# A state-space scan and a mixture of experts on one core: dt's sum moves to TensorE, an eighth of one product to GpSimd, and the set-up is reordered

## The chip, the core and the metric

One core of a Trainium2 chip runs the whole program in one launch. The metric is device time in microseconds, from the program's start to its end. The engines are TensorE (PE), VectorE (DVE), ScalarE (ACT), GpSimd (POOL) and SyncE (SP, which only issues DMAs). Each runs its own instruction stream in program order; they meet at semaphores.

## What is computed

The input x is 16 sequences of 1024 tokens with 256 features. The output is x plus a selective state-space scan plus a mixture of 8 experts, both on the layer-normalised x.

```python
dt = softplus(einsum('bsd,ed->bse', x, dt_w) + dt_b)
A = -exp(log_A)
b = einsum('bsd,nd->bsn', x, B_w) + B_b      # 32 states
c = einsum('bsd,nd->bsn', x, C_w) + C_b
def step(h, inp):
    x_t, dt_t, b_t, c_t = inp
    A_bar = exp(A[None] * dt_t[..., None])
    h = A_bar * h + (dt_t * x_t)[..., None] * b_t[:, None, :]
    y = einsum('bdn,bn->bd', h, c_t) + D_skip * x_t
    return (h, y)
...
out = relu(einsum('ecd,edh->ech', disp, w1) + b1) ; out = einsum('ech,ehd->ecd', h, w2) + b2
```

Each token goes to its two best experts, up to a capacity of 4096 tokens per expert.

## The kernel before, in words

**Set-up.** The first 125 us normalise all tokens and write them to DRAM (`xn_rows`). Then VectorE finds each token's experts and its place there, and in the stretch from about 168 to 280 us it builds one-hot tiles (`one_hots`, lines L1316 to L1319) that TensorE multiplies into a map of slots to tokens (`map_batch`, L603 and L605). It does so in 32 batches. ScalarE makes the third factor (`low_part`, L848) in the same order, and between the batches it evacuates the projections that the scan's first sequence needs: `evac_prep` waits in `evac_bc` (L826) until the former B and C rows have left `bcv` by a DMA (`store_bc`, semaphore `b_st`). The batches run in a rolled loop on VectorE, and the last two rounds are written out behind it. SyncE then issues twelve loads of 512 KB (dt, dtx, B, C rows) and behind them the next store of `bcv`. GpSimd starts, once the map is ready, with the gather of the first tokens and then makes the first `u`.

**The main loop** has 128 steps; a step makes 1024 tokens' scans for 8 groups of 128 (feature, state) rows, and runs 256 token slots through an expert. Per step:

- VectorE makes 8 scans (L1366, 128x1024 each) and 4 weighing products (`weigh(st, i)`, L1353, 128x2048 each: states times a row of C), in the order scan 0, weigh 0, scan 1, scan 2, weigh 1, scan 3, scan 4, weigh 2, scan 5, scan 6, weigh 3, scan 7.
- GpSimd makes the `u` that the scans take, dtx times B, in four products of two groups each (L1146). Between them stand two gathers of tokens (L1097), two scatters of results (L1109), the sum of dt's two parts zv and zl (`dt_sum`, L1075) and dt times x (`dtx_part`, L1082).
- ScalarE makes 8 decays (L882, exp into a pair of PSUM banks), 4 copies of C's row into PSUM bank 6 (`c_copy(i)`, L966; `c_copy(i)` must end before `weigh(st, i)`), the evacuations of the experts' hidden units (`up_out`, L927) and outputs (`down_out`, L952), the evacuations of the next projections, softplus, gates and tables.
- TensorE makes `moe_up` (L677) in four parts and `moe_down` (L686, L688) in two, sums the weighed states (`quad(i)`, L638), and makes the projections and transposes (L573, L580, L527). In the first step of each four it makes the skip product too (L649), and ScalarE moves y out (L891, L895).

PSUM bank 6 has one user at a time: C's row, the projections, the slots' transpose, the rows' transpose. So each of these waits for the weighing product ahead of it (semaphore `hc_done`), and the next `c_copy` waits for them. Of TensorE's stream in a step, what matters below is its end and its beginning:

```python
moe_down(0)
quad(2)
turn_rows()          # waits hc_done >= 4*st + 5, that is: weigh 3 of this step has ended
if ng == 0:
    skip(1)
moe_down(1)
quad(3)
# next step
moe_up(0)
prepare_bc()
moe_up(1)
```

and of ScalarE's stream, whose order is fixed: `up_out(0)`, `bc_out`, `c_copy(1)`, the gates, a decay, `up_out(1)`, a decay, `up_out(2)`, the table of the gather, `z_out`, `c_copy(2)`, two decays, `up_out(3)`.

## Time and profile before

| what | us |
|---|---|
| median of 3 runs | 3699.03 (3698.89 to 3699.51) |
| the profiled execution, its own time | 3694.47 |
| its span, first to last instruction | 3692.8 |
| mean granted clock of TensorE | 0.985 |

The profiled execution is one of the same kind as the three timed runs, 4.6 us below their median; outside its span lie 1.7 us. A share of busy time is a mean over the set-up (the first 285 us) and the loop, which have different limits.

### The profile page before, as it was taken

To read this page: it belongs to the slowest core of one execution; us is meant where nothing else is said; L and a number is where in the kernel's file an instruction comes from. 1 tells how busy PE (TensorE), PEld (TensorE's weight loads), DVE (VectorE), ACT (ScalarE), POOL (GpSimd) and SP (SyncE) were. 2 spreads that over 40 slices of the span, in tenths; PEclk is the share of its full clock that TensorE was granted. 3 is DMA by queue.
4 is the path that set the end of the run, shared out by engine and by line. 5 is a ranking of instruction groups with operands and counts; after the bars stand their busy time and mean duration, and the time that the engine had idled before them with its cause. 6 is when DMAs were issued, how large, how long until landed. Compare 5 with 4: busy or idle time off the path is not lost.

```text
span 3692.8 us, 61914 instructions
## 1 busy us (share of the span) xinstructions
PE 3039.8 (82%) x16324; PEld 2028.2 (55%) x16324; DVE 3579.7 (97%) x2121; ACT 2645.8 (72%) x5125; POOL 3270.8 (89%) x1331
## 2 busy tenths in 40 slices
PE   4477888888888888888888888888888888888886
PEld 3255555555555555555555555555555555555554
DVE  7778999999999999999999999999999999999998
ACT  6356777777777777777777777777777777777776
POOL 1039999999999999999999999999999999999997
PEclk8799999999999999999999999999999999999999
DMA  9954565665565555655666555555556555555656
GB/s 287 248 148 111 162 172 162 187 169 149 142 188 169 163 167 165 184 154 138 169 186 172 164 166 166 172 141 168 167 180 179 165 161 156 160 172 159 174 164 177
DMA packets 336737, 626.19 MB, mean 170 GB/s; under 512 B 50230, under 2 KB 221389, under 8 KB 336144
## 3 DMA queue, kind: packets, MB, share of 16 engines
q1 hardware_dynamic: 265728, 536.81, 45.1%
q0 software_dynamic: 54272, 85.27, 13.0%
q10 hardware_dynamic: 16400, 0.13, 0.9%
q8 instruction: 149, 2.44, 0.3%
q14 instruction: 188, 1.54, 0.1%
HBM read 513.60 MB, written 125.78 MB: 173 GB/s over the span
## 4 chain that ended last, share of the span: by engine, by line
issue 30%; PE 25%; DVE 14%; ACT 12%; POOL 11%; DMA 5%; ACTq 1%; SPq 1%; DVEq 0%; POOLq 0%
PE bank L677 10%; PE bank L686 8%; POOL u L1146 7%; DVE h L1366 6%; DVE hc L1353 6%; ACT bank L882 4%; ACT ht L927 3%; PE bank L638 2%; DMA dtx<-dtx_rows 2%; POOL xg L1097 2%; POOL out_rows L1109 1%; PE bank L527 1%; ACT gate L971 1%; ACT zv L821 1%; DMA dt<-x 1%
## 5 line engine op out<-in xcount | busy, mean ns | idle before, releaser
L1146 POOL TENSOR_TENSOR u<-dtx,b_sb 128x2048 f32<-128x2048 f32 x512 | 2429.9, 4746 | 35.5 <-DMA dtx<-dtx_rows 22.3
L1366 DVE TENSOR_TENSOR_SCAN h<-bank,u 128x1024 f32<-128x1024 f32 x1024 | 2287.6, 2271 | 18.3 <-POOL u L1146 16.0
L882 ACT ACTIVATE bank<-dt,a_neg 128x1024 f32<-128x1024 f32 x1026 | 1128.2, 1107 | 194.2 <-DVE h L1366 188.3
L677 PE MATMUL bank<-xgt,w_sb 128*128 128x256 f32 x4096 | 1013.0, 390 | 231.7 <-ACT ht L927 229.2
L1353 DVE TENSOR_TENSOR hc<-h,bank 128x2048 f32<-128x2048 f32 x514 | 1161.5, 2260 | 8.5 <-ACT bank L966 6.6
L677 PEld LDWEIGHTS bank<-xgt,w_sb 128*128 128x128 f32 x4096 | 739.4, 190 | 574.9 <-issue 494.3
L686 PE MATMUL bank<-w_sb,ht 128*128 128x256 f32 x4096 | 934.6, 381 | 0.0
L686 PEld LDWEIGHTS bank<-w_sb,ht 128*128 128x128 f32 x4096 | 760.6, 190 | 113.3 <-issue 15.3
L927 ACT ACTIVATE ht<-bank,b_sb 128x256 f32<-128x256 f32 x1024 | 422.8, 463 | 318.8 <-PE bank L677 314.3
L638 PE MATMUL bank<-hc,rsum 128*32 128x512 f32 x4112 | 547.6, 605 | 1.3 <-DVE hc L1353 1.3
L1109 POOL DMA_INDIRECT out_rows<-o_sb,sidx x258 | 416.4, 1614 | 52.7 <-issue 37.4
L966 ACT ACTIVATE bank<-c_sb 128x512 f32<-128x512 f32 x512 | 303.0, 592 | 31.7 <-ACT bcv L826 3.2
L1097 POOL DMA_INDIRECT xg<-xn_rows,gidx x256 | 272.4, 1064 | 60.1 <-issue 57.5
L1082 POOL TENSOR_TENSOR dtx_n<-dt_n,xnt 128x256 f32<-128x256 f32 x137 | 128.9, 941 | 218.4 <-DVE dt_n L1257 192.1
L527 PE MATMUL bank<-ident,xg 128*128 128x128 f32 x516 | 85.0, 288 | 138.1 <-DVE hc L1353 131.1
L527 PEld LDWEIGHTS bank<-ident,xg 128*128 128x128 f32 x516 | 54.5, 141 | 254.5 <-DVE hc L1353 247.2
L952 ACT ACTIVATE o_sb<-bank,gate 128x256 f32<-128x256 f32 x256 | 118.8, 464 | 101.8 <-PE bank L688 101.8
L527 PE MATMUL bank<-ident,xr 128*128 128x128 f32 x256 | 52.4, 286 | 144.3 <-DVE hc L1353 144.3
L527 PEld LDWEIGHTS bank<-ident,xr 128*128 128x128 f32 x256 | 25.7, 140 | 256.8 <-issue 256.8
L638 PEld LDWEIGHTS bank<-hc,rsum 128*32 128x32 f32 x4112 | 80.9, 108 | 131.7 <-issue 98.6
L573 PEld LDWEIGHTS bank<-xnt,dtw 128*128 128x128 f32 x1104 | 143.1, 193 | 6.2 <-issue 1.0
L573 PE MATMUL bank<-xnt,dtw 128*128 128x128 f32 (+1 forms) x1104 | 146.4, 276 | 0.0
(130 smaller groups left out, 1954.7 us busy)
## 6 DMA issues: line engine op xcount, KB each, us to landing
b_sb<-bc_rows SPq DMA_DIRECT2D x258, 512.0 KB, 4.3
c_sb<-bc_rows SPq DMA_DIRECT2D x258, 512.0 KB
dt<-dt_rows SPq DMA_DIRECT2D x132, 512.0 KB, 6.5
dtx<-dtx_rows SPq DMA_DIRECT2D x132, 512.0 KB, 7.0
w_sb<-w SPq DMA_DIRECT2D x18, 1024.0 KB, 5.4
dt_rows<-dt_n SPq DMA_DIRECT2D x137, 128.0 KB, 3.9
dtx_rows<-dtx_n SPq DMA_DIRECT2D x137, 128.0 KB
dt<-x SPq DMA_DIRECT2D x33, 512.0 KB, 5.6
```

The lines of the kernel that those rows point to most:

```text
L573: mm = pe.matmul(z_ps[:, g * Q:(g + 1) * Q], dtw[:, k, g * P:(g + 1) * P], src, start=(k == 0), stop=(k == KD - 1))
L638: mm = pe.matmul(y_ps[c * RD:(c + 1) * RD, th, :], rsum[:], hc[:, GPP * th + c, :], start=False, stop=True, skip_group_check=True, tile_po ...
L677: mm = pe.matmul(m_ps[:, c, :], w1_sb[:, kk, ch * P:(ch + 1) * P], xgt[:, kk, :], start=(kk == 0), stop=(kk == KD - 1))
L686: pe.matmul(m_ps[:, j, :], ht[:, c, j * P:(j + 1) * P], w2_sb[:, c, :], start=(c == 0), stop=False)
L882: act.activation(a_ps[k % 2], dt[:, k % GPP, :], ACT.Exp, scale=a_neg[:, col:col + 1]).then_inc(a_ready, 1)
L927: ins = act.activation(ht[:, ch, :], m_ps[:, c, :], ACT.Relu, bias=b1_sb[:, bass.ds(ex * HC + ch, 1)])
L966: act.activation(c_ps, c_sb[:, j, th * HALF:(th + 1) * HALF], ACT.Copy).then_inc(c_ready, 1)
L1097: pool.indirect_dma_start(xg[:, buf, j, :], None, xn_d, rows, bounds_check=T - 1, oob_is_err=False).then_inc(xg_in, 16)
L1109: pool.indirect_dma_start(outf, rows, o_sb[:, buf, j, :], None, bounds_check=T - 1, oob_is_err=False, compute_op=ALU.add).then_inc(o_scatt ...
L1146: pool.tensor_tensor(u[:, gp:gp + 2, :], dtx[:, gp:gp + 2, :], b_sb[:, j, :].unsqueeze(1).to_broadcast([P, 2, S]), ALU.mult).then_inc(u_re ...
L1353: dve.tensor_tensor(hc[:, GPP * th:GPP * (th + 1), :], h[:, GPP * j:GPP * (j + 1), th * HALF:(th + 1) * HALF], c_ps.unsqueeze(1).to_broadc ...
L1366: dve.tensor_tensor_scan(h[:, k, :], a_ps[k % 2], u[:, k % UB, :], 0.0, ALU.mult, ALU.add).then_inc(scan_done, 1)
```

## The change

- **dt's sum.** GpSimd's `dt_sum` leaves the loop. TensorE multiplies zv and then zl by the identity into 256 columns of bank 6 (`sum_dt`), and ScalarE copies the sum to `dt_n` (`dt_out`). `log_part` stands one place earlier on ScalarE, so that zl is there. In TensorE's stream `turn_rows` and `sum_dt` now stand ahead of `quad(2)`, since ScalarE takes both out of the bank together before `c_copy(0)`.
- **One product with C.** Of the fourth weighing product's 2048 columns VectorE makes 1536 and then 256 in an instruction of its own, GpSimd the other 256 (`part_product`), straight from the C row in SBUF. `quad(3)`, the next step's scan 3 and the next load of that C row wait for it (`part_done`).
- **The set-up.** VectorE's map loop is written out. The store of `bcv` stands ahead of the twelve loads, whose order changes. The first `u` product is made as soon as the one-hot tiles are free, ahead of the first gather; in the loop the first pair of a step is issued at the end of the step before. One `dt_sum` stands before the loop.
- **SyncE.** `load_rows` stands at the step's end.

```diff
@@ -413,16 +417,19 @@
             sp.wait_ge(dtx_free, 1)
-            for gp in range(GPP):
+            sp.wait_ge(bcv_done, NG + 1)
+            store_bc(NG, 1, 0)
+            load_dtx(0, 0, 0)
+            load_dtx(0, 0, 1)
+            load_b(0, 0)
+            load_dt(0, 0, 0)
+            load_dt(0, 0, 1)
+            load_c(1, 1)
+            for gp in (2, 3):
                 load_dt(0, 0, gp)
                 load_dtx(0, 0, gp)
-                if gp == 0:
-                    load_b(0, 0)
-                    load_c(1, 1)
             load_b(1, 1)
             load_c(0, 0)
-            sp.wait_ge(bcv_done, NG + 1)
-            store_bc(NG, 1, 0)
...
                     def quad(i):
                         pe.wait_ge(hc_done, st * 4 + i + 2)
+                        if i == 3:
+                            pe.wait_ge(part_done, st + 2)
                         sum_states(i % 2)
...
+                    def sum_dt():
+                        pe.wait_ge(l_done, NG + 2 + st + 1)
+                        for src in (zv, zl):
+                            mm = pe.matmul(sum_ps, ident[:], src[:, s % 2].rearrange("p k t -> p (k t)"),
+                                           start=(src is zv), stop=(src is zl), skip_group_check=True)
+                        mm.then_inc(dt_filled, 1)
...
                     moe_down(0)
+                    turn_rows()
+                    sum_dt()
                     quad(2)
-                    turn_rows()
                     if ng == 0:
                         skip(1)
                     moe_down(1)
...
+                    def dt_out():
+                        act.wait_ge(dt_st, 16 * p + 1)
+                        act.wait_ge(prep_done, p + 1)
+                        settle(act)
+                        act.activation(dt_n[:].rearrange("p k t -> p (k t)"), sum_ps, ACT.Copy).then_inc(dt_done, 1)
...
                         if k == 7:
                             rows_turned()
+                            dt_out()
...
                         if k == 5:
+                            log_part(p, s % 2)
...
                         if k == 6:
                             down_out(0)
-                            log_part(p, s % 2)
...
+            def part_product(st):
+
+                pool.wait_ge(c_in[0], 16 * (st + 1))
+                pool.wait_ge(nsum_done, 4 * st + 2 + NSUM0)
+                settle(pool)
+                pool.tensor_tensor(hc[:, 2 * GPP - 1, PW:HALF], h[:, GPP - 1, HALF + PW:S], c_sb[:, 0, HALF + PW:S],
+                                   ALU.mult).then_inc(part_done, 1)
+
+            pool.wait_ge(oh_used, 2 * NT // OHB + 2)
+            pool.wait_ge(b_in[0], 16)
+            for g in (0, 1):
+                pool.wait_ge(dtx_in[g], 16)
+            make_u(0, 0)
...
                         if m == 1:
-                            dt_sum(NG + 1 + st, (s + 1) % 2)
                             dtx_part(NG + 1 + st, (b + 1 + (s + 1) // NG) % 2, (s + 1) % NG)
-                        if m >= 2:
+                        if m == 3:
+                            part_product(st)
...
-            with long_loop(dve, NG // 2 - 1) as qq:
-                for i in range(2):
-                    one_hots(qq * 2 + i)
-                    prep_dt(qq * 2 + i + 2, i)
-            one_hots(NG - 2)
-            prep_dt(NG, 0)
-            one_hots(NG - 1)
+            for q in range(NG):
+                one_hots(q)
+                if q < NG - 1:
+                    prep_dt(q + 2, q % 2)
...
+                if i == 3:
+                    dve.tensor_tensor(hc[:, GPP:2 * GPP - 1, :], h[:, 0:GPP - 1, HALF:S],
+                                      c_ps.unsqueeze(1).to_broadcast([P, GPP - 1, HALF]), ALU.mult)
+                    dve.tensor_tensor(hc[:, 2 * GPP - 1, 0:PW], h[:, GPP - 1, HALF:HALF + PW], c_ps[:, 0:PW],
+                                      ALU.mult).then_inc(hc_done, 1)
+                    return
```

TensorE's stream from `moe_down(0)` of one step (first row) to `moe_down(1)`, in the kernel before; `xr` are the rows that `turn_rows` transposes, `hc` with `rsum` is a `quad`, and the word in brackets is the semaphore that a row waits for:

```order
L686 MATMUL bank<-w_sb,ht 128x256 [waits evac_done]
L686 MATMUL bank<-w_sb,ht 128x256 x7
L688 MATMUL bank<-b_parts,ones_h 128x256
L638 MATMUL bank<-hc,rsum 32x512 [waits hc_done]
L638 MATMUL bank<-hc,rsum 32x512 x3
L709 ISA
L710 REGISTER_ALU [waits xr_in0]
L527 MATMUL bank<-ident,xr 128x128 [waits hc_done]
L527 MATMUL bank<-ident,xr 128x128
L666 REGISTER_ALU
L686 MATMUL bank<-w_sb,ht 128x256 [waits evac_done]
```

The same place in the changed kernel (its lines are some ten higher):

```order
L698 MATMUL bank<-b_parts,ones_h 128x256
L721 ISA
L722 REGISTER_ALU [waits xr_in0]
L537 MATMUL bank<-ident,xr 128x128 [waits hc_done]
L537 MATMUL bank<-ident,xr 128x128
L729 REGISTER_ALU
L731 MATMUL bank<-zv,ident 128x256 [waits l_done]
L731 MATMUL bank<-zl,ident 128x256
L648 MATMUL bank<-hc,rsum 32x512 [waits hc_done]
L648 MATMUL bank<-hc,rsum 32x512 x3
L676 REGISTER_ALU
L696 MATMUL bank<-w_sb,ht 128x256 [waits evac_done]
```

The `quad(2)` has moved from ahead of the transposes, and so ahead of their wait for `hc_done`, to behind it, and the two products for dt are new between them.

SyncE's stream at the end of the set-up, before (the last four of the twelve loads, and what stands behind them):

```order
L364 DMA dt<-dt_rows 128x1x1024
L364 DMA dtx<-dtx_rows 128x1x1024
L353 DMA b_sb<-bc_rows 128x1x1024
L353 DMA c_sb<-bc_rows 128x1x1024
L373 DMA bc_rows<-bcv 64x128 [waits bcv_done]
L381 DMA dt_rows<-dt_n 128x2x128 [waits dt_done]
```

and in the changed kernel:

```order
L390 DMA dtx_rows<-dtx_n 128x2x128 [waits prep_done]
L377 DMA bc_rows<-bcv 64x128 [waits dtx_free,dtx_st,bcv_done,dt_st,b_st]
L368 DMA dtx<-dtx_rows 128x1x1024 x2
L357 DMA b_sb<-bc_rows 128x1x1024
L368 DMA dt<-dt_rows 128x1x1024 x2
L357 DMA c_sb<-bc_rows 128x1x1024
```

The store of `bcv` (`bc_rows<-bcv`) has moved from behind the twelve loads to ahead of them.

## Rows read from the trace of the kernel before

**Rows 1.** The page: the span, and part 1, each engine's busy time

```profile
span 3692.8 us, 61914 instructions
...
PE 3039.8 (82%) x16324; PEld 2028.2 (55%) x16324; DVE 3579.7 (97%) x2121; ACT 2645.8 (72%) x5125; POOL 3270.8 (89%) x1331
```

**Rows 2.** The page, part 5: line engine op, out<-in | busy, mean ns | idle

```profile
L1146 POOL TENSOR_TENSOR u<-dtx,b_sb 128x2048 f32<-128x2048 f32 x512 | 2429.9, 4746 | 35.5 <-DMA dtx<-dtx_rows 22.3
...
L1353 DVE TENSOR_TENSOR hc<-h,bank 128x2048 f32<-128x2048 f32 x514 | 1161.5, 2260 | 8.5 <-ACT bank L966 6.6
```

**Rows 3.** Timeline of VectorE, first and last step: start, us, engine, line, out<-in

```profile
308.16 2.26 DVE L1353 TENSOR_TENSOR hc<-h,bank 128x2048 f32<-128x2048 f32 x1
...
3666.09 2.26 DVE L1353 TENSOR_TENSOR hc<-h,bank 128x2048 f32<-128x2048 f32 x1
```

**Rows 4.** Timeline of VectorE, one plain step, its weighing products

```profile
1846.11 2.26 DVE L1353 TENSOR_TENSOR hc<-h,bank 128x2048 f32<-128x2048 f32 x1
...
1865.79 2.26 DVE L1353 TENSOR_TENSOR hc<-h,bank 128x2048 f32<-128x2048 f32 x1
...
1872.35 2.26 DVE L1353 TENSOR_TENSOR hc<-h,bank 128x2048 f32<-128x2048 f32 x1
```

**Rows 5.** Timeline of TensorE, the same step

```profile
1846.11 1.06 PE L638 MATMUL bank<-hc,rsum 128*32 128x512 f32 x8
1848.51 0.41 PE L527 MATMUL bank<-ident,xr 128*128 128x128 f32 x2 [1.33 <-DVE hc L1353]
1848.76 3.69 PE L686 MATMUL bank<-w_sb,ht 128*128 128x256 f32 x16
...
1852.59 1.06 PE L638 MATMUL bank<-hc,rsum 128*32 128x512 f32 x8
1853.58 1.99 PE L677 MATMUL bank<-xgt,w_sb 128*128 128x256 f32 x8
```

**Rows 6.** Timeline of ScalarE, the same step

```profile
1850.60 1.12 ACT L882 ACTIVATE bank<-dt,a_neg 128x1024 f32<-128x1024 f32 x1 [1.17 <-DVE h L1366]
...
1855.72 0.84 ACT L927 ACTIVATE ht<-bank,b_sb 128x256 f32<-128x256 f32 x2 [1.36 <-PE bank L677]
...
1864.36 0.60 ACT L966 ACTIVATE bank<-c_sb 128x512 f32<-128x512 f32 x1
```

**Rows 7.** Timeline of TensorE, a step after a skip product

```profile
1901.24 1.09 PE L649 MATMUL bank<-xnt,dskip_m 128*128 128x512 f32 x2
```

**Rows 8.** Timeline of ScalarE, the third copy of C in steps 60, 61

```profile
1891.01 0.60 ACT L966 ACTIVATE bank<-c_sb 128x512 f32<-128x512 f32 x1
...
1917.70 0.60 ACT L966 ACTIVATE bank<-c_sb 128x512 f32<-128x512 f32 x1
```

**Rows 9.** Timeline of VectorE, end of step 60 and third product of 61

```profile
1898.59 2.26 DVE L1353 TENSOR_TENSOR hc<-h,bank 128x2048 f32<-128x2048 f32 x1
...
1918.42 2.29 DVE L1353 TENSOR_TENSOR hc<-h,bank 128x2048 f32<-128x2048 f32 x1
```

**Rows 10.** Groups of GpSimd by line, 300 to 3600 us

```profile
L1082 POOL TENSOR_TENSOR dtx_n<-dt_n,xnt 128x256 f32<-128x256 f32 x125 | 90.7, 725 | 25.6 <-POOL dt_n L1075 25.6
L1075 POOL TENSOR_TENSOR dt_n<-zv,zl 128x256 f32<-128x256 f32 x125 | 90.6, 725 | 0.4
```

**Rows 11.** Timeline of VectorE while the map is made

```profile
175.67 0.69 DVE L1316 TENSOR_TENSOR u<-iota_pair,prt_h 128x1024 bf16<-128x1024 bf16 x1 [8.02 <-issue]
...
271.36 0.69 DVE L1316 TENSOR_TENSOR u<-iota_pair,prt_h 128x1024 bf16<-128x1024 bf16 x1 [13.97 <-PE bank L605]
```

**Rows 12.** Timeline of ScalarE, the same stretch

```profile
266.39 0.36 ACT L826 ACTIVATE bcv<-bank,bcb 64x128 f32<-64x128 f32 x1 [12.79 <-DMA bc_rows<-bcv]
```

**Rows 13.** Timeline of GpSimd, the first gather

```profile
278.43 1.12 POOL L1124 DMA_INDIRECT xg<-xn_rows,slot_tok  x1 [23.46 <-issue]
```

**Rows 14.** Groups of GpSimd by line, 176 to 246 us

```profile
L1082 POOL TENSOR_TENSOR dtx_n<-dt_n,xnt 128x256 f32<-128x256 f32 x6 | 29.5, 4918 | 49.0 <-DVE dt_n L1257 49.0
```

**Rows 15.** Windows: each engine's busy us (count), PEclk, DMA share, GB/s

```profile
320.00:340.00 20.00, 14.76 (x68) 10.73 (x66) 14.32 (x7) 12.53 (x25) 15.64 (x8) 0.83 0.48 121
```

More of the change, by code:

```diff
@@ L201, in ssm_moe @@
         rows_done = sem("rows_done")
+        dt_filled = sem("dt_filled")
+        part_done = sem("part_done")
         wg_ready = sem("wg_ready")
@@ L275, in ssm_moe @@
         GV = G // 2
+        PW = HALF // 2
         NBASE = B
@@ L470, in next_c @@
                         settle(sp)
+                        if j == 0:
+                            sp.wait_ge(part_done, st + 2)
+                            settle(sp)
                         load_c(j, 2 * st + 2 - j)
@@ L502, in _ @@
                         next_dt(3)
+                    sp.wait_ge(xr_turned, st + 1)
+                    settle(sp)
+                    load_rows((s + 1) % 2, (b + 1 + (s % SPS + 4) // NG) % B, (s + 4) % NG)
                     if s == SPE - 1 - ROT:
@@ L958, in c_copy @@
                             act.wait_ge(rows_done, st + 2)
+                            act.wait_ge(dt_done, p + 2)
                             act.wait_ge(c_in[1], 16 * (st + 2))
@@ L1046, in _ @@
         def _(pool):
[L1047 removed]
+            start_at_one(pool, u_ready, prep_done, part_done)
             pool.memset(o_sb[:], 0.0).then_inc(zeroed, 1)
@@ L1118, in add_y, with make_u @@
                                y_rows[:, h0:h1], accum_op=ALU.add).then_inc(y_out, 16)
+            def make_u(jb, gp):
+                pool.tensor_tensor(u[:, gp:gp + 2, :], dtx[:, gp:gp + 2, :],
+                                   b_sb[:, jb, :].unsqueeze(1).to_broadcast([P, 2, S]), ALU.mult).then_inc(u_ready, 1)
+            def part_product(st):
[9 more added lines that the diff above has]
+            make_u(0, 0)
             pool.wait_ge(gates_out, 16)
@@ L1127, in _ @@
             pool.tensor_copy(sidx[:], slot_dst[:, 0:SJ]).then_inc(sidx_done, 1)
+            dt_sum(NG + 1, 1)
             pool.wait_ge(base_out, 16 * NBASE)
@@ L1137, in _ @@
                     adds = gh == 0 and ng == 1
-                    for m in range(NPR):
-                        j, gp = m // 2, 2 * (m % 2)
-                        if gp == 0:
-                            pool.wait_ge(b_in[j], 16 * (st + 1))
-                        if ng == 0 and m < 2:
-                            for g in (gp, gp + 1):
-                                pool.wait_ge(dtx_in[g], 16 * (hf + 1))
-                        pool.wait_ge(scan_done, st * NG + 2 * m + 1 - UB + 1 + SCAN0)
-                        pool.tensor_tensor(u[:, gp:gp + 2, :], dtx[:, gp:gp + 2, :],
-                                           b_sb[:, j, :].unsqueeze(1).to_broadcast([P, 2, S]), ALU.mult).then_inc(u_ready, 1)
+                    for m in range(NPR + 1):
+                        j, gp = m // 2 % 2, 2 * (m % 2)
+                        sn, stn = (s + 1, st + 1) if m == NPR else (s, st)
+                        if m:
+                            if gp == 0:
+                                pool.wait_ge(b_in[j], 16 * (stn + 1))
+                            if sn % HPB == 0 and m in (1, NPR):
+                                for g in (gp, gp + 1):
+                                    pool.wait_ge(dtx_in[g], 16 * (2 * b + sn // HPB + 1))
+                            pool.wait_ge(scan_done, st * NG + 2 * m + 1 - UB + 1 + SCAN0)
+                            make_u(j, gp)
                         if m == 0 and adds:
@@ L1363, in _ @@
                     dve.wait_ge(a_ready, st * NG + k + 2)
+                    if k == GPP - 1:
+                        dve.wait_ge(part_done, st + 1)
                     if k % GPP == 0:
```

11 lines of the change are left out of this document (5 added, 6 removed).

## The prediction

> **What bounds the kernel now.** I read the page first: the shares of busy time and the costliest groups. VectorE is busy 3579.7 of 3692.8 us and GpSimd 3270.8 [rows 1], so one of these two seems to set the pace. Second, the timeline of VectorE over the loop: from the fourth weighing product of the first step to that of the last lie 3666.09 - 308.16 us and 127 steps, 26.44 us a step [rows 3]. In a plain step it is 1872.35 - 1846.11 = 26.24 us, with twelve instructions end to end, so 2.19 us from start to start of one [rows 4]. So in plain steps VectorE is the bound, and the 0.20 us that the mean lies above comes from a few steps where something else is late.
>
> Third, and this decides the case, the other engines' timelines over that plain step, read from one instant: T = 1848.37, where the fourth weighing product ends (1846.11 + 2.26) [rows 4]. TensorE stands idle 1.33 us for it, transposes the rows at 1848.51, goes on with `moe_down(1)` at 1848.76, `quad(3)` at 1852.59 and the next step's `moe_up(0)` at 1853.58 [rows 5]. ScalarE is idle 1.36 us until that gives it something to evacuate, at 1855.72 [rows 6]. From there its work is a fixed sequence of busy pieces and of waits for TensorE's next part, up to the third copy of C, which ends at 1864.36 + 0.60 = 1864.96, that is T + 16.59 [rows 6]. The third weighing product needs it and starts at 1865.79, T + 17.42 [rows 4]. The margin seems 0.83 us.
>
> The trace holds its own test of that margin. Step 60 has a skip product (1.09 us) between the transposes and `moe_down(1)` [rows 7]. There T is 1898.59 + 2.26 = 1900.85, the copy of C in the step after ends at 1918.30, T + 17.45, and the product starts at 1918.42 [rows 8, 9]: T + 17.57 in place of T + 17.42, 0.12 behind the copy. So work added to TensorE behind T comes out at VectorE as soon as it exceeds 0.83 - 0.12 = 0.71 us. In step 60 itself, where ScalarE also moves y, the copy ends at 1891.61; with T = 1872.35 + 2.26 = 1874.61 that is T + 17.00 [rows 4, 8].
>
> **The change part by part.**
>
> *TensorE behind T: +1.95 us a step.* `quad(2)` filled TensorE's wait: it ran at 1846.11, ahead of the 1.33 us of idle time [rows 5]. Now it stands behind the transposes, whose wait has not changed, so it costs its full start-to-start time, 1853.58 - 1852.59 = 0.99 us, as `quad(3)` shows [rows 5]. `sum_dt` is two products with 256 moving columns in float32. The nearest row is `moe_up(0)`: four such products (eight records) in 1.99 us, the last record's tail counted [rows 5], so at most 0.50 each; `moe_down(1)` has eight in 3.69, 0.46 each. I take 0.96 for two (0.92 to 1.00). The transposes themselves stay. Sum 0.99 + 0.96 = 1.95 (1.9 to 2.1 with the wait for one more semaphore, which no row prices; the 0.12 above bounds it).
>
> *VectorE: -0.21 us a step.* The fourth product loses 256 of 2048 columns, an eighth of 2.19, 0.27 us, and becomes two instructions. The second one costs between nothing and what 2.26 busy against 2.19 of pace leaves, about 0.07; I take 0.06, and the gain is between 0.20 and 0.27.
>
> *The new step.* Plain: the copy ends at T + 16.59 + 1.95 = T + 18.54, the third product starts 0.12 later, and from there to the next T were 1874.61 - 1865.79 = 8.82 us [rows 4], now 8.61. Sum 27.27. After a skip product: 17.45 + 1.95 + 0.12 + 8.61 = 28.13. In the step with y's copies: 17.00 + 1.95 + 0.12 + 8.61 = 27.68. Of four steps two are plain: mean (2 x 27.27 + 28.13 + 27.68) / 4 = 27.59. The sum assumes that the delay repeats in every step; it does, for T itself is the end of VectorE's product, and TensorE waits for it again. Before, the mean was 26.44. So +1.15 us a step, times 128, 147 us; and a single stall of 20 - 14.32 = 5.7 us between 320 and 340 us [rows 15], which the mean of before holds and my sum over steps doesn't, stays: **+153 us**.
>
> *GpSimd: hidden.* It loses `dt_sum`, 0.73 us and the 25.6 / 125 = 0.20 us that `dtx_part` waited for it, and gains `part_product`, also 256 columns from SBUF, priced by the same rows at 0.73 [rows 10]; two more waits may take 0.1 to 0.3. With at most 3270.8 / 128 = 25.6 us busy a step [rows 1] in a step that now takes 27.6, it has room. `part_product` follows the fourth `u` and is due only at `quad(3)`, 6 us behind the next T; should it be later than that, every microsecond would count.
>
> *ScalarE: hidden.* `rows_turned` starts 0.96 us later and `dt_out` adds a copy like the one of C (0.60 for twice the columns), say 0.4. Ahead of the decay that follows, 1.17 us were idle [rows 6]. So that decay and the first copy of C come some 0.2 to 0.3 later, and VectorE will wait in this step for the third copy anyway. If the cover were gone it would cost those 0.3. `log_part` moves within idle time.
>
> *SyncE: nothing.* The row load is needed a step later; the loads of dtx move up by one issue; the load of C waits for `part_product` and has most of a step to land.
>
> *The set-up: -15 us (-7 to -19).* ScalarE waits 12.79 us for the store of `bcv` behind the loads, and VectorE 13.97 us at its last batch for the consequence [rows 11, 12]. With the store ahead of the loads, both all but go, and the map is ready some 13.4 us earlier, midway between the two. But the first gather, at 278.43 [rows 13], now stands behind a `u` product of 4.75 us [rows 2], and TensorE's first step hangs on the gather: GpSimd used to wait for the rest of the map, which covers part of it, so between 8.6 and 13.4 us are gained, and I take 11. Then VectorE's 8.02 us at the entry of the rolled loop, with no other engine to wait for [rows 11]: written out, the code may lose all or none of it, and I take 4.
>
> Against this speaks the trace's price for GpSimd beside VectorE: in the map stretch a 256-column product takes 4.92 us, in the loop 0.73 [rows 10, 14]. The early `u` runs beside the map's arithmetic on VectorE; if it is held up as that product was, by 4.2 us, the gather comes as much later, and the set-up gains 11 in place of 15. The Trainium skill (SBUF — State Buffer, "Who interferes with whom" and "SBUF: two separate sides") has the reason: the two engines share a port pair that one instruction holds to its end, and VectorE takes part in that with two SBUF inputs. In the loop one input of VectorE's scans and products is in PSUM, and by that rule `part_product` is free there, as `dtx_part`'s 0.73 us agrees.
>
> *Sum.* 3694.5 + 153 - 15 = 3832.5 for the profiled execution; the median of the runs lay 4.5 above that, so **3837 us**, 3.7% slower.
>
> **The rivals.**
>
> *A. The chain from T does not bind, and VectorE sets the pace as before: faster.* Then a plain step takes 26.24 - 0.21 = 26.03, GpSimd with at most 25.6 busy stays just below, and the mean falls from 26.44 to about 26.1: -43, with the set-up -58, 3641 us. For it: VectorE is 97% busy. Against it: step 60's skip product already used up the margin [rows 7 to 9]. It decides if TensorE's added work behind T stays under 0.71 us in a plain step; this needs less than half of what I count. 8%.
>
> *B. Part of the 1.95 us is absorbed,* for instance because TensorE's two products overlap with the sums' weight loads, or ScalarE's waits between the parts of `moe_up` give way. If 1.2 of it count in place of 1.95, the steps take 0.75 less than forecast, the loop costs 96 less, and the time is 3741. The rigid row of ScalarE's pieces speaks against it. 8%.
>
> *C. TensorE's clock falls.* Its idle time ahead of the transposes grows from 1.33 us to about 2.2. In the one loop stretch where it paused long, 320 to 340 us, TensorE was busy 14.76 of 20 us and the granted clock was 0.83 in the mean, a mixture of 2.4 and 1.2 GHz [rows 15]. If in each step half of the 8.5 us that TensorE works behind T ran at 1.2 GHz, the step would take 4 us more, and the kernel some 4350. A plain step with two pauses of 1.3 us kept its full clock, so I give it 3%. The Trainium skill (TensorE: Matmul & The Clock Gate, "What's actually happening") says that the throttled state is the default and activity lifts it, which is why a longer pause is the thing to watch.
>
> *D. The forecast,* 79%. A result within 0.2% would need A and B to meet by accident: 2%.
>
> **How the numbers follow.** The forecast's own range: 0.25 us a step either way is 32 us, and the set-up's ends are 4 and 8, so 3800 to 3875. To hold 8 in 10 it needs little more; B reaches in from below, and I take 3785 to 3880. Slower by over 0.2% (what a measurement of this kernel can tell from no change): D, C, B, 0.90; within: 0.02; faster: 0.08.
>
> **What would show it.** The step in VectorE's timeline is about 27.3 to 28.1 us. VectorE idles some 1.2 us a step, nearly all ahead of the third weighing product, put down to the copy of C. TensorE's idle time for the fourth product is near 2.2 us; its two new products take 0.96 us; GpSimd's new product takes 0.73 us, and GpSimd now waits for VectorE's scans. ScalarE's wait for the store of `bcv` at 253 us is gone. If VectorE's idle time were ahead of `weigh` 0 instead, the two copies on ScalarE would be what I mis-sized; if steps were 26.1 us, the chain from T would be wrong altogether.

## The result, and the profile of the changed kernel

| | median us (lowest to highest) | ratio, 95% interval |
|---|---|---|
| before, 4 runs beside the changed kernel | 3699.27 (3698.89 to 3700.31) | |
| changed, 4 runs | 3907.73 (3898.54 to 3913.71) | 1.0561 (1.0543 to 1.0579) |

The change makes the kernel 5.6% slower, 208 us. The direction is the forecast's; the size is 71 us above 3837 and 28 above the range's upper end. The profiled execution took 3913.71 us. Its runs also lie 15 us apart, those of before 1.4. First the page of the changed kernel: span, busy time, and three groups (busy, mean ns | idle before and its releaser).

```profile
span 3912.0 us, 63978 instructions
...
PE 3231.4 (83%) x16836; PEld 2136.7 (55%) x16836; DVE 3598.8 (92%) x2249; ACT 2679.9 (69%) x5253; POOL 3267.5 (84%) x1333
...
L1152 POOL TENSOR_TENSOR u<-dtx,b_sb 128x2048 f32<-128x2048 f32 x513 | 2336.7, 4555 | 253.4 <-DVE h L1421 224.8
...
L1407 DVE TENSOR_TENSOR hc<-h,bank 128x2048 f32<-128x2048 f32 x386 | 880.0, 2280 | 183.7 <-ACT bank L995 182.3
...
L537 PE MATMUL bank<-ident,xr 128*128 128x128 f32 x256 | 53.5, 292 | 231.5 <-DVE hc L1404 231.5
```

VectorE was 97% busy [rows 1] and is 92% busy: it now waits 183.7 us, nearly all for ScalarE's copies of C (8.5 before [rows 2]). GpSimd waits for VectorE's scans, where it hardly waited for anything [rows 2]. TensorE stands 231.5 us before the 128 transposes, 1.81 us each. These are signs that the prediction named.

VectorE's timeline over one plain step of the changed kernel (start, us):

```profile
2051.45 1.73 DVE L1402 TENSOR_TENSOR hc<-h,bank 128x1536 f32<-128x1536 f32 x1
2053.10 0.41 DVE L1404 TENSOR_TENSOR hc<-h,bank 128x256 f32<-128x256 f32 x1
2053.43 4.46 DVE L1421 TENSOR_TENSOR_SCAN h<-bank,u 128x1024 f32<-128x1024 f32 x2
...
2064.70 2.29 DVE L1407 TENSOR_TENSOR hc<-h,bank 128x2048 f32<-128x2048 f32 x1 [0.24 <-ACT bank L995]
...
2072.23 2.29 DVE L1407 TENSOR_TENSOR hc<-h,bank 128x2048 f32<-128x2048 f32 x1 [0.70 <-ACT bank L995]
...
2078.82 1.73 DVE L1402 TENSOR_TENSOR hc<-h,bank 128x1536 f32<-128x1536 f32 x1
2080.46 0.41 DVE L1404 TENSOR_TENSOR hc<-h,bank 128x256 f32<-128x256 f32 x1
```

TensorE's, and two rows of ScalarE's, in the same step:

```profile
2053.66 0.41 PE L537 MATMUL bank<-ident,xr 128*128 128x128 f32 x2 [2.03 <-DVE hc L1404]
2053.91 0.60 PE L731 MATMUL bank<-zv,ident 128*128 128x256 f32 x2
2054.34 0.59 PE L731 MATMUL bank<-zl,ident 128*128 128x256 f32 x2
2054.87 1.07 PE L648 MATMUL bank<-hc,rsum 128*32 128x512 f32 x8
2055.87 3.72 PE L696 MATMUL bank<-w_sb,ht 128*128 128x256 f32 x16
...
2059.73 1.07 PE L648 MATMUL bank<-hc,rsum 128*32 128x512 f32 x8
2060.72 1.99 PE L687 MATMUL bank<-xgt,w_sb 128*128 128x256 f32 x8
```

```profile
2062.86 0.84 ACT L947 ACTIVATE ht<-bank,b_sb 128x256 f32<-128x256 f32 x2 [1.35 <-PE bank L687]
...
2071.51 0.60 ACT L995 ACTIVATE bank<-c_sb 128x512 f32<-128x512 f32 x1
```

T, the end of the fourth product, is 2053.10 + 0.41 = 2053.51. `moe_down(1)` starts at T + 2.36; before it was T + 0.39 [rows 4, 5]. The third copy of C ends at 2072.11, T + 18.60 (before T + 16.59 [rows 6]), and the third weighing product starts 0.12 behind it, at T + 18.72 in place of T + 17.42. So what was added to TensorE behind T, 1.97 us, arrives at VectorE whole, less the margin; 0.24 us of VectorE's waiting lies ahead of the second product already. The next T is 2080.87: the step takes 27.36 us. Of the 35 plain steps with the clock whole, 32 have `moe_down(1)` at this place; in the other three it comes up to 0.17 us later.

**What no term of the forecast held** is the clock. From the first transposes to the last, 127 steps of the changed kernel take 28.193 us each, more than any kind of clean step explains: plain 27.37 and 27.45 in the mean, with y's copies 27.90, after a skip product 28.22, together 27.735. The rest is 33 steps that hold a stretch at a granted clock of 0.5: the first step, which had one before too, and 32 others that take 28.9 to 29.7 us; 25 of them are the step that follows the long one behind a skip product. One is at 1911. Windows of the changed kernel (length, busy us of PE, PEld, DVE, ACT, POOL, PEclk, DMA share, GB/s), two in that step and one at the same place of the clean step above, then TensorE's and VectorE's rows:

```profile
1911.00:1915.50 4.50, 3.64 (x16) 1.59 (x17) 4.50 (x4) 2.49 (x5) 4.01 (x4) 0.75 0.38 129
1915.50:1920.00 4.50, 4.50 (x21) 3.28 (x23) 4.50 (x3) 0.31 (x2) 4.50 (x2) 0.87 0.08 25
2052.80:2057.30 4.50, 3.64 (x21) 2.29 (x22) 4.50 (x4) 2.49 (x5) 4.01 (x4) 1.00 0.33 100
```

```profile
1911.86 0.41 PE L537 MATMUL bank<-ident,xr 128*128 128x128 f32 x2 [2.04 <-DVE hc L1404]
...
1913.07 1.84 PE L648 MATMUL bank<-hc,rsum 128*32 128x512 f32 x8
1914.84 4.59 PE L696 MATMUL bank<-w_sb,ht 128*128 128x256 f32 x16
```

```profile
1921.45 2.29 DVE L1421 TENSOR_TENSOR_SCAN h<-bank,u 128x1024 f32<-128x1024 f32 x1 [0.97 <-ACT bank L902]
...
1924.54 2.29 DVE L1407 TENSOR_TENSOR hc<-h,bank 128x2048 f32<-128x2048 f32 x1 [0.80 <-ACT bank L995]
```

In the clean step the sum and `moe_down(1)` took 1.07 and 3.72 us; here 1.84 and 4.59, in all 1.64 more, behind an idle time of 2.04 us. Part of TensorE's work ran at 1.2 GHz, on the chain from T, so the step takes 29.28. All of it in the loop: (28.193 - 27.735) x 127 = 58 us, of which before had 5.7 in one step. By the Trainium skill (TensorE: Matmul & The Clock Gate, "What's actually happening") activity releases the throttle, and its lack brings it back; that the fall comes right behind the engine's longest idle time agrees. In all 32 steps it begins within 1.7 us of the transposes that end a wait of 2.03 or 2.04 us; but only 32 of the loop's 94 waits of that length are followed by one.

**The set-up.** The loop's first transposes come at 303.51 us, before at 310.56: 7 us gained. The changed kernel, VectorE's and then GpSimd's timeline:

```profile
174.07 0.69 DVE L1366 TENSOR_TENSOR u<-iota_pair,prt_h 128x1024 bf16<-128x1024 bf16 x1 [0.15 <-DVEq L1354]
...
193.81 0.69 DVE L1366 TENSOR_TENSOR u<-iota_pair,prt_h 128x1024 bf16<-128x1024 bf16 x1 [8.88 <-issue]
...
269.16 3.78 DVE L1381 CAST slot_tok<-map_f 128x256 int32<-128x256 f32 x1
```

```profile
268.29 4.50 POOL L1152 TENSOR_TENSOR u<-dtx,b_sb 128x2048 f32<-128x2048 f32 x1 [6.77 <-PE bank L615]
274.29 1.13 POOL L1172 DMA_INDIRECT xg<-xn_rows,slot_tok  x1 [1.50 <-issue]
```

and the same cast in the kernel before:

```profile
276.78 0.29 DVE L1333 CAST slot_tok<-map_f 128x256 int32<-128x256 f32 x1
```

The two waits behind the store of `bcv` [rows 11, 12] are gone. The stall of 8.02 us at the loop's entry [rows 11] is gone too, but written out the map has one of 8.88 us ahead of its fifth batch. The cast at 269.16 takes 3.78 us beside GpSimd's early `u`, 0.29 before. So it was VectorE that was held there and not GpSimd, whose product took 4.50. With the 13.97 us wait for the store down to 0.46, entry and new stall nearly cancelling, and 1.4 us of faster batches, the map is 13.9 us shorter (from 167.65, where the entry stall began, to 276.78; now from 173.92 to 269.16). Of the 3.5 us that the cast takes longer little reaches the loop: from the cast's start to the first transposes are 34.35 us, before 33.78, so 0.6. The work ahead of the map ended 6.3 us later than in the profile of before; the same cast stands at 263.9 and at 269.7 us in two experiments below with this map code, so single profiles differ by that much here. These are the 7 us: 13.9 less 6.3 less 0.6. No run isolates the store's move; its 13.5 us are the two waits that went.

### The profile page after: what moved, and what is told of

It reads as the page before. It is cut to its first block, busy times and chain, and to the rows that moved or that the text cites. A ratio compares the mean times of both kernels' runs of the same rounds, so it can differ in the third digit from the quotient of the medians.

```text
span 3912.0 us, 63978 instructions
## 1 busy us (share of the span) xinstructions
PE 3231.4 (83%) x16836; PEld 2136.7 (55%) x16836; DVE 3598.8 (92%) x2249; ACT 2679.9 (69%) x5253; POOL 3267.5 (84%) x1333
## 4 chain that ended last, share of the span: by engine, by line
PE 42%; issue 20%; ACT 17%; DVE 15%; ACTq 2%; DMA 1%; DVEq 1%; POOL 0%; SPq 0%; POOLq 0%
PE bank L687 14%; PE bank L696 12%; DVE h L1421 11%; PE bank L648 8%; ACT bank L902 6%; ACT ht L947 5%; PE bank L731 3%; PE bank L537 2%; ACT zv L841 2%; ACT gate L1000 2%; DVE hc L1404 1%; PE bank L659 1%; DMA dt<-x 1%; ACT bcv L846 1%; ACT gate L1006 1%
## 5 line engine op out<-in xcount | busy, mean ns | idle before, releaser
L1152 POOL TENSOR_TENSOR u<-dtx,b_sb 128x2048 f32<-128x2048 f32 x513 | 2336.7, 4555 | 253.4 <-DVE h L1421 224.8
L1407 DVE TENSOR_TENSOR hc<-h,bank 128x2048 f32<-128x2048 f32 x386 | 880.0, 2280 | 183.7 <-ACT bank L995 182.3
L696 PE MATMUL bank<-w_sb,ht 128*128 128x256 f32 x4096 | 963.7, 389 | 0.0
L696 PEld LDWEIGHTS bank<-w_sb,ht 128*128 128x128 f32 x4096 | 775.4, 194 | 222.8 <-issue 118.8
L648 PE MATMUL bank<-hc,rsum 128*32 128x512 f32 x4112 | 571.1, 629 | 0.2 <-DVE hc L1407 0.2
L537 PE MATMUL bank<-ident,xr 128*128 128x128 f32 x256 | 53.5, 292 | 231.5 <-DVE hc L1404 231.5
L1402 DVE TENSOR_TENSOR hc<-h,bank 128x1536 f32<-128x1536 f32 x128 | 221.3, 1729 | 0.0
L967 ACT ACTIVATE xnt<-bank 128x256 f32<-128x256 f32 x128 | 49.2, 384 | 250.2 <-PE bank L731 239.3
```

Source lines behind the costliest of these rows:

```text
L537: return pe.matmul(dst, src, ident[:], start=start, stop=True, is_transpose=True, skip_group_check=True)
L648: mm = pe.matmul(y_ps[c * RD:(c + 1) * RD, th, :], rsum[:], hc[:, GPP * th + c, :], start=False, stop=True, skip_group_check=True, tile_po ...
L696: pe.matmul(m_ps[:, j, :], ht[:, c, j * P:(j + 1) * P], w2_sb[:, c, :], start=(c == 0), stop=False)
L1152: pool.tensor_tensor(u[:, gp:gp + 2, :], dtx[:, gp:gp + 2, :], b_sb[:, jb, :].unsqueeze(1).to_broadcast([P, 2, S]), ALU.mult).then_inc(u_r ...
L1407: dve.tensor_tensor(hc[:, GPP * th:GPP * (th + 1), :], h[:, GPP * j:GPP * (j + 1), th * HALF:(th + 1) * HALF], c_ps.unsqueeze(1).to_broadc ...
```

## The experiments

Each ratio is to runs of the kernel before on the same chip: its medians were 3701.55 us (e1 to e4), 3698.02 (e5 to e8) and 3697.30 (e9 to e12). A step is the mean over 127 in the profile, from transposes to transposes; in these profiles before has 26.44, changed 28.19. A difference of a few us between medians of two groups is no more than the chips' own.

**e1_quad_ahead**: the changed kernel, with `quad(2)` back in TensorE's wait.

```diff
                     moe_down(0)
+                    quad(2)
                     turn_rows()
                     sum_dt()
-                    quad(2)
```

> The changed kernel with quad(2) put back ahead of turn_rows; sum_dt stays behind the transposes. Theory (the chain of TensorE and ScalarE work behind T, the end of the fourth weighing product, sets the step): 0.99 us less stands behind T, so a plain step takes about 26.4 us, one after a skip product 27.2, one with y's copies 26.8, mean 26.6 to 26.8 in place of 28.19. TensorE's idle time ahead of the transposes falls back to 1.2 us and its granted clock stays whole in the loop. Time 3700 to 3735 us. Rival (the new waits on part_done, or ScalarE's two copies, set the step): the order on TensorE does not matter and the time stays above 3850 us.

Measured 3711.66 us, ratio 1.0023 (1.0014 to 1.0033), a step of 26.64, and besides the first step only one with a fall of the clock. The place of four matmuls is worth 196 us of the 208: clean steps give 27.735 - 26.58 = 1.155 us each, 147 us, and the clock most of the rest. dt's sum alone behind T puts `moe_down(1)` at T + 1.26, 0.87 us later than before, and the plain steps take 26.16 to 26.27, less than the 26.4 that I expected.

**e2_wait_filled**: the changed kernel, and TensorE fills its wait with three products whose result is overwritten.

```diff
                         free(FD + j)
+                        if j == 0:
+                            for c in range(3):
+                                pe.matmul(m_ps[:, j, :], ht[:, c, 0:P], w2_sb[:, c, :], start=(c == 0), stop=(c == 2))
```

> The changed kernel with three more products of 256 columns ahead of moe_down(0), into the same PSUM columns, which the real products then overwrite: 1.4 us of work in place of idle time ahead of the transposes. Theory (the clock's share): the granted clock no longer falls once in four steps, those steps take 27.4 in place of 29.1 us, and the time falls by about 50 us, to 3850 to 3865 us. Rival 1 (the clock's falls cost nothing, since they lie in a margin): no change, 3900 to 3915 us. Rival 2 (the added products come out on the path): slower than 3915 us.

Measured 3866.90 us, 2 above the expected range, ratio 1.0437 (1.0419 to 1.0454), a step of 27.81. No step holds a stretch at 1.2 GHz, and the clean steps nearly keep their length (those with y's copies take 28.11 for 27.90). TensorE does more work, waits less ahead of the transposes, and the kernel is 41 us faster than the changed one (46 by the two ratios). One step of e2, TensorE:

```profile
1919.59 0.41 PE L537 MATMUL bank<-ident,xr 128*128 128x128 f32 x2 [0.74 <-DVE hc L1407]
```

So the clock's share comes with TensorE's idle time and not from the work added: with that time filled the falls are gone.

**e3_quad_behind**: the kernel before, with this one move.

```diff
                     moe_down(0)
-                    quad(2)
                     turn_rows()
+                    quad(2)
```

> The kernel before with quad(2) moved behind turn_rows and nothing else. Theory (chain behind T): 0.99 us more behind T against a margin of 0.71 us in plain steps; plain step 26.5, after a skip product 27.4, with y's copies 26.9, mean 26.85, so +50 us: 3750 us with the clock whole, and up to 3800 us if TensorE's longer idle time (2.3 us) takes the clock down once in four steps as in the changed kernel. Rival (quad(2) is free wherever it stands, because TensorE has idle time in each step): within 3 us of 3699.

Measured 3862.32 us, ratio 1.0416 (1.0398 to 1.0433): far above what I expected. Clean steps are 26.74 to 27.74, but 48 falls stand in the 127 steps. Groups of TensorE, 400 to 3600 us, before and then in e3 (two records to a pair of transposes):

```profile
L527 PE MATMUL bank<-ident,xr 128*128 128x128 f32 x242 | 49.5, 286 | 135.9 <-DVE hc L1353 135.9
```

```profile
L527 PE MATMUL bank<-ident,xr 128*128 128x128 f32 x230 | 53.7, 320 | 230.7 <-DVE hc L1353 230.7
```

A transpose pair waits 135.9 / 121 = 1.12 us before and 230.7 / 115 = 2.01 in e3. Without the sum of dt's parts TensorE is idle longer than in the changed kernel (1.80 in that stretch), and its clock falls oftener. In a clean plain step `moe_down(1)` starts at T + 1.48, 1.09 us later than before, and the step takes 26.72 to 26.89.

**e4_setup_only**: the changed kernel with the loop's work as before: dt's sum on GpSimd, the whole fourth product on VectorE, `quad(2)` ahead.

```diff
-                    turn_rows()
-                    sum_dt()
                     quad(2)
+                    turn_rows()
...
+                            dt_sum(NG + 1 + st, (s + 1) % 2)
...
-                        if m == 3:
-                            part_product(st)
```

> The changed kernel with dt's sum back on GpSimd in the loop, all of the fourth product on VectorE and TensorE's old order: what is left is the set-up (store of bcv ahead of the loads, map loop written out, first u early), the u pair issued a step earlier, log_part one place earlier and the row load at the step's end. Theory: the first scan comes 10 us or more earlier than at 286.3 us and the loop takes 26.44 us a step as before, so 3684 to 3692 us. Rival (the early u holds up VectorE's map as much as the rest gains, or the moved u pair costs in the loop): 3697 us or more.

Measured 3682.62 us, ratio 0.9943 (0.9927 to 0.9960): this part of the change alone makes the kernel faster. Its step of 26.41 is almost that of before (the 0.03 us between them is 3 us), and its first transposes come at 304.38, 6.2 us earlier. So the gain that the profiles show is mostly the set-up's. They hold only half of the 19 us between the medians: the profile of before, at 3694.47, was 7 us faster than its median here, and where that lies is not known.

**e5_dt_only** is e1 without `part_product`; **e6_dt_on_pool** is e4 with `part_product`.

> The changed kernel with quad(2) ahead of the transposes, as in e1_quad_ahead, and without part_product: VectorE makes the whole fourth weighing product again. What is left of the change is the sum of dt by TensorE and ScalarE, and the set-up. With e4_setup_only (neither), e6_dt_on_pool (the part product alone) and e1_quad_ahead (both) it makes a square of four. Theory (the chain behind T binds, T being the end of the fourth product): sum_dt adds 0.96 us to a chain that had 0.71 to spare, and VectorE's share ahead of T is 0.2 longer than in e1, so a step takes up to 0.2 more than e1's 26.64: 26.8 to 26.85, and the time is 3730 to 3738. Rival (GpSimd's new product and its waits hold up e1's steps): without it the steps are no longer than e1's, 3700 to 3712.

> The changed kernel with dt's sum back on GpSimd and TensorE's and ScalarE's order of before: of the loop's changes only the part product on GpSimd is left. TensorE's chain is that of before, so nothing but VectorE and GpSimd can set the pace: VectorE would need 26.03 us a step, GpSimd carries 0.73 us more than before, 26.3 us or more with its waits. Theory (GpSimd has room only because dt's sum has left it): GpSimd becomes the bound, a step takes 26.6 to 26.9, and the time is 3710 to 3745, slower than e4_setup_only at 3683. Rival (the part product is pure gain wherever GpSimd is below VectorE): 26.2 a step, 3655.

| step, us | whole product on VectorE | an eighth on GpSimd |
|---|---|---|
| dt's sum on GpSimd | 26.41 (e4, 3682.62 us) | 26.95 (e6, 3755.24) |
| dt's sum on TensorE | 26.82 (e5, 3735.18) | 26.64 (e1, 3711.66) |

e5: ratio 1.0100 (1.0083 to 1.0117); e6: 1.0154 (1.0137 to 1.0171), 10 us above my range. The part product alone costs 0.54 us a step, and with dt's sum gone from GpSimd it gains 0.18. Groups of e6, 400 to 3600 us, GpSimd's `u` and VectorE's scan:

```profile
L1147 POOL TENSOR_TENSOR u<-dtx,b_sb 128x2048 f32<-128x2048 f32 x476 | 2297.3, 4826 | 2.8
```

```profile
L1416 DVE TENSOR_TENSOR_SCAN h<-bank,u 128x1024 f32<-128x1024 f32 x951 | 2149.5, 2280 | 77.6 <-POOL u L1147 68.4
```

GpSimd's `u` waits for nothing, and VectorE's scans wait for it: GpSimd is the bound. So the two halves of the loop's change belong together, but with `quad(2)` in its old place they are still 29 us slower than neither.

**e7_split2**: the changed kernel with as much of TensorE's work ahead of the transposes as fits.

```diff
                     moe_down(0)
+                    quad(2)
+                    free(FD + 1)
+                    down_products(1, range(2))    # two of moe_down(1)'s eight
                     turn_rows()
                     sum_dt()
-                    quad(2)
...
+                        if k == 6:
+                            down_out(0)           # ahead of the decay, not behind
```

**e8_split4** is the same with four products.

> The changed kernel with three things moved: quad(2) ahead of the transposes, the first two products of moe_down(1) ahead of them too, and on ScalarE down_out(0) ahead of the decay of group 6 in place of behind it, so that the bank is free for them. The work is the same, and 0.92 us more of it lies in TensorE's wait. Theory: the chain behind T is 1.95 - 0.99 - 0.92 = 0.04 us longer than in the kernel before, so it no longer binds, and VectorE or GpSimd sets the pace at 26.03 to 26.3; no stretch of the loop at 1.2 GHz; 3640 to 3675, faster than e1 (3712) and e4 (3683). Rival (e1's 26.64 a step comes from GpSimd, not from the chain behind T): no gain over e1, 3705 to 3715.

> As e7_split2, with four products of moe_down(1) ahead of the transposes in place of two: 1.84 us of work ahead of a wait that leaves TensorE some 1.2 us. Theory: the transposes come up to 0.6 us after T, and what hangs on them (ScalarE's copies out of bank 6, the first copy of C, the weighing product of group 0) comes later, while the end of the chain gains nothing more over e7: 0 to 0.4 us a step more than e7, 3660 to 3710. Rival (only the length of the chain from moe_down(1) on counts): as e7 or up to 10 us faster.

Measured: e7 3670.62 us, ratio 0.9926 (0.9909 to 0.9943), a step of 26.32 and plain steps of 26.04, which is VectorE's own work; e8 3706.98, ratio 1.0032 (1.0019 to 1.0046), a step of 26.49 in its profile, whose execution of 3694.30 us was the fastest of ten. Groups of e7, 400 to 3600 us:

```profile
L537 PE MATMUL bank<-ident,xr 128*128 128x128 f32 x244 | 49.1, 283 | 4.2
```

```profile
L1412 DVE TENSOR_TENSOR hc<-h,bank 128x2048 f32<-128x2048 f32 x365 | 826.7, 2265 | 20.6 <-ACT bank L1000 20.3
```

TensorE no longer waits before the transposes, and e7 beats both the kernel before and the changed one. In e8, at the end of a step with y's copies:

```profile
2006.88 2.29 DVE L1412 TENSOR_TENSOR hc<-h,bank 128x2048 f32<-128x2048 f32 x1 [1.08 <-ACT bank L1000]
```

This is the first weighing product behind T. It waits for the first copy of C, which stands on ScalarE behind what the transposes give it, and they now come late: in a plain step 0.77 us behind T, in e7 0.15. In e7 the same wait was 0.21 us (below, at 1992.37). The plain steps of e8 are 26.23. By the medians, twice as much ahead of the wait is 36 us worse, by the profiles 24; e8's nine other executions are slower than the profiled one and had a lower mean granted clock, 0.974 to 0.980 for its 0.983. The wait was worth filling, not overfilling.

**e9_setup_split**: e7's split on e4, so without the loop's change.

```diff
                     quad(2)
+                    free(FD + 1)
+                    down_products(1, range(2))
                     turn_rows()
```

> e4_setup_only (set-up of the changed kernel, loop of the kernel before) with the split of e7_split2: down_out(0) earlier on ScalarE and two products of moe_down(1) ahead of the transposes. It tells whether the loop's change (dt's sum, the part product) is worth anything once the chain behind T has room. Theory: with the split e4's chain is 0.92 us shorter and leaves VectorE alone as the bound, 26.24 us a plain step against e7's 26.04, little above it in the steps with y's copies: mean 26.25 to 26.32 against e4's 26.41, and the time is 3662 to 3672, the same as e7's 3671 within 10 us. Rival (e4's excess over 26.24 isn't the chain): 3680 to 3686, no gain over e4, and e7's loop change is worth its full 0.2 us a step.

Measured 3673.54 us, ratio 0.9942 (0.9924 to 0.9961), a step of 26.34: within 3 us of e7 by the medians and 6 by the ratios, which come from two chips; the intervals overlap, and the time is 1.5 us above the expected range. Against e4 the ratios are equal (0.9942 and 0.9943) and the medians 9 us apart, so the split's own gain on this loop is not settled either; beside e11 and e12, e4's near copies on the same chip, it is 7 us. With the chain behind T shortened, the new sharing-out of work among the engines gains nothing that this measurement tells apart.

**e10_y_behind**: e7, and ScalarE's copy of y behind the third copy of C.

```diff
                         if k == 3:
                             z_out()
                             c_copy(2)
+                            if ng == 0:
+                                y_up(0, 1 - gh, 2 * hf + 1)      # was at k == 2
```

> e7_split2 with one more move on ScalarE, in the step of each four that moves y out: y_up(0) stands behind c_copy(2) in place of ahead of it. In e7 that step takes 26.6 to 26.8 us (28 in some) against 26.04 of a plain one, and VectorE waits 1.3 us for c_copy(2) there. Theory (ScalarE's 0.5 to 0.6 us ahead of that copy is on the chain): those 32 steps get up to 0.5 us shorter, 5 to 16 us, and the time is 3654 to 3667. Rival (the wait only moves to c_copy(3), which then comes later): 3668 to 3673, as e7.

Measured 3677.53 us, ratio 0.9949 (0.9933 to 0.9966), 7 us above e7 by the medians, on another chip, and 10 above the expected range. A step is 26.38 in the mean, e7's 26.32, and those with y's copies and the clock whole got longer, 27.12 for 26.90: a miss. VectorE's waiting products of one step with y's copies, in e7 and in e10:

```profile
1979.13 2.29 DVE L1412 TENSOR_TENSOR hc<-h,bank 128x2048 f32<-128x2048 f32 x1 [1.32 <-ACT bank L1000]
1992.37 2.29 DVE L1412 TENSOR_TENSOR hc<-h,bank 128x2048 f32<-128x2048 f32 x1 [0.21 <-ACT bank L1000]
```

```profile
1980.17 2.29 DVE L1412 TENSOR_TENSOR hc<-h,bank 128x2048 f32<-128x2048 f32 x1 [0.72 <-ACT bank L1000]
1993.90 2.29 DVE L1412 TENSOR_TENSOR hc<-h,bank 128x2048 f32<-128x2048 f32 x1 [0.70 <-ACT bank L1000]
```

The wait of 1.32 us fell by 0.60, and the next one rose by 0.49: it moved on. In this step it went to the next step's first copy of C, not to c_copy(3) as the rival had it.

**e11_u_late** is e4 with the first `u` behind the first gather; **e12_rolled** is e4 with VectorE's map loop rolled.

```diff
-            make_u(0, 0)
             ...   # the first gather
+            make_u(0, 0)
```

```diff
-            for q in range(NG):
-                one_hots(q)
+            with long_loop(dve, NG // 2 - 1) as qq:
+                for i in range(2):
+                    one_hots(qq * 2 + i)
```

> e4_setup_only with the first u product behind the first gather, where the kernel before has it. In e4 that product (4.5 us) runs beside VectorE's map arithmetic, whose first instruction with SBUF operands alone took 3.8 us beside it in place of 0.3. Theory (the two held each other up, and the gather stood behind the product): that instruction takes 0.3 us again, the first gather starts 3 to 4.5 us earlier, the first transposes of the loop 2 to 4 us earlier, while the first scan comes 1 to 3 us later; as the first step hangs on the gather, the time is 0 to 4 us below e4's 3683. Rival (the instruction's 3.8 us has another cause): it takes 3.8 again, and nothing is gained but the place of the gather.

> e4_setup_only with VectorE's map loop rolled again, as in the kernel before. Theory: the 8 us at the loop's entry come back on VectorE at about 168 us, and all behind it comes 5 to 8 us later: 3687 to 3691 against e4's 3683, first scan at 281 to 285 in place of 276.7. Rival (the stall was covered by ScalarE and TensorE, which VectorE waited for later): the first scan stays within 2 us of e4's.

Measured 3680.70 us (0.9958, 0.9942 to 0.9975) and 3680.49 us (0.9952, 0.9934 to 0.9969), both the same as e4 within their scatter. For e11 that is inside what I expected, for e12 it is 7 us below: a miss. In e11, VectorE and GpSimd:

```profile
265.33 0.29 DVE L1368 CAST slot_tok<-map_f 128x256 int32<-128x256 f32 x1
```

```profile
266.98 1.13 POOL L1157 DMA_INDIRECT xg<-xn_rows,slot_tok  x1 [9.29 <-issue]
```

The cast takes 0.29 us again, and the gather follows its start by 1.65 us in place of 5.13. This agrees with the rule of the Trainium skill (SBUF — State Buffer, "Who interferes with whom"), which counts a cast among the operations that can take the port pair shared with GpSimd. But from the cast to the first transposes e11 has 33.75 us and e4 34.68: 0.9 gained. In e12, VectorE:

```profile
180.58 0.69 DVE L1354 TENSOR_TENSOR u<-iota_pair,prt_h 128x1024 bf16<-128x1024 bf16 x1 [6.72 <-issue]
```

The entry's stall is back, and the map's other waits `<-issue` are all under 0.3 us; e4 has 10.59 us `<-issue` at 194.33 instead. The first scan comes at 273.94, no later than e4's 276.68. Writing the loop out moved the stall and gained nothing; its cause is not settled. Both kinds stand where VectorE comes to instructions that it hasn't run before, but so do most batches of the written-out loop that don't stall.

## Why the prediction was right in kind and wrong in size

- **The chain from T binds.** Right: e1, e3 and e7 move work across that one wait and the time follows. Rival A is refuted.
- **The term "TensorE behind T, +1.95 us a step"** measured 1.97 at `moe_down(1)` and 2.01 at the third copy of C: dt's two products take 0.96 (2054.87 - 2053.91), as priced, and `quad(2)` 1.00. None of it is absorbed, so rival B is refuted as well. Alone behind the transposes the two parts cost 0.87 (e1) and 1.09 us (e3), so the price of each by itself was off by a tenth, and their sum right.
- **VectorE, -0.21**: 2053.43 - 2051.45 = 1.98 against 2.19, to the hundredth. GpSimd's product: 0.73 us, as priced.
- **The new steps**: plain 27.36 in most and 27.39 in the mean for 27.27, with y's copies 27.90 for 27.68, after a skip product 28.22 for 28.13. The mean of clean steps is 27.735 for 27.59, which is 18 us over the loop. In the plain step shown, 0.06 of it is the copy of C and 0.03 the way from the third product to the next T.
- **The failed step is rival C, "TensorE's clock falls".** It was priced only for every step, at 4 us each, and set aside with 3% since "a plain step with two pauses of 1.3 us kept its full clock". What happened lies between: 32 of the 127 steps besides the first, 1.6 us each, in all 52 us more than the 5.7 that the forecast kept. Without these 52 us the median would lie at 3856, inside the range. My own text had the pause growing to 2.2 us, beyond anything that a plain step of before had shown. That was the place for a term with a bound, not for a rival of all or nothing.
- **The term "set-up -15"** measured -7. The two waits behind the store gave 13.5 us, for 13.4 priced. The 4 us for the loop's entry were nothing, since the stall moved (e12: rolled again, it came back at its old place). The early `u` was to cost 2.4 by the first gather and 4 more in the lower case; it held VectorE's cast for 3.5 and was not held itself, and cost 0.6 ahead of the loop (0.9 between e4 and e11). The map's later start in that profile, 6.3, took the rest. By its runs e4's part of the change did better: its ratio makes it 21 us (15 to 27), of which some 3 are the loop's.

For the profiled execution: 18 (chain) + 52 (clock) + 8 (set-up) + 4 (tail behind the last transposes), less 1 for 127 steps in place of 128, is the 81 us between 3832.5 and 3913.7.

## What to carry to other kernels

On an engine that waits once in a period for another, what stands ahead of the wait is free and what stands behind it is paid in full beyond the margin: read the wait first, fill it (e7), and don't overfill it (e8). If an edit lengthens an idle time of TensorE beyond what the trace has shown at full clock, give the clock a term of its own with two ends, and not only a case for every step; look at the longest single idle time wherever it stands in the step. A change of several parts is worth splitting: here one part gained 0.6%, and the rest hid it, most of it through one misplaced call.

## What the runs showed that I had not expected

- The same fall of the clock costs or not by where it stands. e6 and e9 have 22 steps each with a stretch at 1.2 GHz, though their transposes of the rows wait only 0.8 and 0.2 us in the mean. In e9's 20 such plain steps VectorE takes 26.25 us, as in the others: another bound hid them. In e6 its 12 plain steps are at most 0.14 us longer than their like. Nine others are longer, 28.5 against 26.8 to 27.0, but VectorE waits for `u` there (2.6 us in the one at 518), and the step at 949 takes 28.8 without a fall.
- What comes ahead of the falls is a long single idle time of TensorE, anywhere in the step. In e9 it stands ahead of the slots' transposes (`ident,xg`), not of the rows':

```profile
692.96 0.66 PE L534 MATMUL bank<-ident,xg 128*128 128x128 f32 x4 [1.98 <-DVE hc L1394]
693.46 5.31 PE L690 MATMUL bank<-w_sb,ht 128*128 128x256 f32 x16
```

| kernel | longest idle time that recurs, us | of these, followed by a fall |
|---|---|---|
| before | 1.31 to 1.47, mostly rows and slots | 0 of 131 |
| e8 | 1.87 to 1.91, slots | 2 of 56 |
| e9 | 1.97 to 2.03, slots | 20 of 45 |
| changed | 2.03 to 2.04, rows | 32 of 94 |
| e3 | 2.23 to 2.24, rows | 46 of 94 |

Behind the first step the 14 profiles hold 127 falls; 121 begin between 0.8 us ahead of the end of a single idle time of 1.79 us or more and 2.5 us behind it, the other six behind two waits close together (0.95 to 1.53 and then 0.62 or 0.63 us). Why one such wait is followed by a fall and the next is not stays open.
- Kernels with many falls that bind also scatter more: 15 us over 4 runs of the changed kernel, 37 over 6 runs of e3, 2.2 over 4 runs of e7. In e3 the two longest executions (3888 and 3892 us) had a mean granted clock of 0.959 and 0.958, the other four 0.963 to 0.966. e8, with three falls in its profile, scattered by 27 over 10 runs, and there too the longer ones had the lower clock (0.983 at 3694 us, 0.974 to 0.976 at 3715 to 3721).
